# Value products in two halves per tile, and groups of heads that run into each other

## The reference

```
x = x + Attention(layernorm(x));  x = x + FFN(layernorm(x))
Attention: q, k, v from x @ Wqkv + b
  y_softmax = softmax(q k^T / sqrt(16) + causal mask) v        per head, 4096 x 4096
  state_t = retention * state_{t-1} + Gamma * (v_t k_t^T)      a 16 x 16 state per head
  y_stp_t = (W_static + state_t) q_t
  alpha = sigmoid(gelu(x @ gate_w1 + b) @ gate_w2 + b)
  y = alpha * y_softmax + (1 - alpha) * y_stp;  out = y @ out_w + out_b
FFN: fp8-rounded activations and weights, one 256 x 256 product, scale, bias
```

## Time and profile before

| | us |
|---|---|
| median of 3 runs (1871.87 to 1874.48) | 1872.21 |
| profiled execution | 1872.81 |
| its span | 1871.0 |
| TensorE: matmuls in flight | 1672.0 (89%) |
| VectorE busy | 1534.8 (82%) |
| ScalarE busy | 1366.0 (73%) |
| GpSimd busy | 1186.3 (63%) |
| maxima, L1401 | 1215.9 |
| exponentials, L1353 | 1124.3 |
| value products, L1262 | 340.2 + 229.8 |

### The profile page before, as it was taken

One profiled execution on the slowest core, in us unless ns is written; L12 is line 12 of the kernel. 1 busy time (PEld: TensorE's weight loads), 2 busy tenths in 40 slices (PEclk: granted clock), 3 DMA queues, 4 the chain that ended last, 5 costly groups with the idle time before them and its releaser, 6 DMA issues. The chain is left out here.

```text
span 1871.0 us, 37359 instructions
## 1 busy us (share of the span) xinstructions
PE 1672.0 (89%) x13712; PEld 598.9 (32%) x13712; DVE 1534.8 (82%) x1717; ACT 1366.0 (73%) x2835; POOL 1186.3 (63%) x1138
## 2 busy tenths in 40 slices
PE   4997589999999999999999999999999999997745
PEld 2553122232333323223333232233333332322632
DVE  3557888999889899998888999988989999831777
ACT  1552178888888788888877888888878888897333
POOL 2100487777777677777777777777778888770620
PEclk9997589999999999999999999999999999999875
DMA  2774442323123422231224222312341321201702
GB/s 78 234 248 145 111 101 62 82 67 90 57 70 81 102 62 80 66 92 56 69 78 108 62 80 66 92 57 67 81 108 60 94 73 49 74 5 28 256 8 83
DMA packets 115321, 162.75 MB, mean 87 GB/s; under 512 B 30081, under 2 KB 57793, under 8 KB 115137
## 3 DMA queue, kind: packets, MB, share of 16 engines
q1 hardware_dynamic: 112608, 158.74, 29.2%
q10 hardware_dynamic: 2528, 1.64, 0.3%
HBM read 121.87 MB, written 38.01 MB: 85 GB/s over the span
## 5 line engine op out<-in xcount | busy, mean ns | idle before, releaser
L1401 DVE TENSOR_REDUCE pmax<-PS 128x2 f32<-128x1024 f32 (+2 forms) x1120 | 1215.9, 1131 | 131.7 <-PE PS L1205 93.7
L1353 ACT ACTIVATE probs<-PS 128x512 f32<-128x512 f32 (+3 forms) x2304 | 1124.3, 572 | 244.8 <-PE PS L1241 167.4
L1241 PE MATMUL PS<-Q_st,K_st 50*128 50x512 f16 (+3 forms) x1408 | 389.4, 361 | 18.4 <-DVE y_sb L1426 4.8
L1205 PE MATMUL PS<-K_st,Q_st 48*128 48x512 f16 (+3 forms) x1408 | 343.7, 360 | 13.3 <-DVE pmax L1401 11.8
L1262 PE MATMUL PS<-probs,V_g 128*17 128x512 f32 (+3 forms) x2816 | 340.2, 556 | 9.3 <-ACT probs L1353 4.5
L1113 POOL TENSOR_TENSOR v_exp<-v_exp,k_rows 128x512 f32<-128x512 f32 x256 | 320.8, 1280 | 39.1 <-DMA v_exp<-qkv_t 38.5
L1155 POOL TENSOR_TENSOR state<-odd,q_rows 128x514 f32<-128x514 f32 x256 | 281.8, 1133 | 6.1
L1241 PE MATMUL PS<-Q_st,K_first 50*128 50x512 f16 (+3 forms) x896 | 270.6, 378 | 15.7 <-DVE shift L1416 5.2
L1205 PE MATMUL PS<-K_first,Q_st 48*128 48x512 f16 (+1 forms) x832 | 212.4, 399 | 26.0 <-DVE pmax L1401 25.5
L1262 PE MATMUL PS<-probs,V_first 128*17 128x512 f32 (+3 forms) x1792 | 229.8, 585 | 0.0
L1241 PEld LDWEIGHTS PS<-Q_st,K_st 50*128 50x128 f16 x1408 | 105.5, 93 | 369.6 <-ACT probs L1353 306.7
(11 more groups left out here) (170 smaller groups left out, 1460.4 us busy)
## 6 DMA issues: line engine op xcount, KB each, us to landing
v_exp<-qkv_t SPq DMA_DIRECT2D x256, 256.0 KB
qkv_t<-proj SPq DMA_DIRECT2D x24, 512.0 KB, 3.8
qk_parts<-parts SPq DMA_DIRECT2D x16, 512.0 KB, 5.3
Q_st<-qk_parts SPq DMA_DIRECT2D x192, 32.0 KB, 4.0
v_rows<-vaug SPq DMA_DIRECT2D x8, 544.0 KB, 6.1
xin<-x SPq DMA_DIRECT2D x8, 512.0 KB, 6.3
k_rows<-qkv_t SPq DMA_DIRECT2D x16, 256.0 KB, 4.0
q_rows<-qkv_t SPq DMA_DIRECT2D x16, 256.0 KB, 6.0
```

The source lines that it names most:

```text
L1205: mm = pe.matmul(PS[:, bank, 0:width], Q_st[rows, c, pair, j * P:(j + 1) * P], keys[rows, pair, blk * CH:blk * CH + width], start=True, st ...
L1241: mm = pe.matmul(PS[:, bank, 0:CH - r * P], keys[rows, pair, kt * P:(kt + 1) * P], Q_st[rows, c, pair, r * P:CH], start=True, stop=(kt < T ...
L1353: act.activation(probs[:, tile % P_SLOTS, h, 0:CH - r * P], PS[:, step[5], 0:CH - r * P], ACT.Exp, scale=SCORE_SCALE).then_inc(exp_done, 1)
L1401: dve.tensor_reduce(pmax[:, s % 2, pair * TPC + j:GH * TPC:PAIRS * TPC, blk], PS[:, bank:bank + SIDES, 0:width], AX.X, ALU.max).then_inc(m ...
```

## The change

`values` takes a part: 0 is the left 256 columns of the output bank, 1 the right 256, 2 the whole. Plain and scan tiles issue part 0 (`v`) after two scores and two maxima and part 1 (`w`) at the end; burst and lag tiles keep the whole product (`V`). The product is still that of the tile before (`V_LAG` is 1). Only part 0 or the whole waits for the exponentials and for the output bank, and only part 1 or the whole signals; in diagonal tiles a half with no columns issues nothing. The units' steps (U) stand first in a plain tile, no longer behind the first scores. `group_steps` takes what is pending from the group before and hands on its own; only the last group runs dry. SyncE's loop now holds only groups 1 and 2, and turns are counted through the whole program.

```diff
+V_LAG = 1
+WHOLE = 2
-PLAIN_TILE = "SUMMSSMMSV"
+PLAIN_TILE = "USSMMvSSMMw"
 BURST_TILE = "USSMMRMMSSMMV"
-SCAN_TILE = "USSMMRSSV"
+SCAN_TILE = "USSRvSSMMw"
 LAG_TILE = "USSMMVSSMMR"
...
-def group_steps(last):
-    steps, turns, pending = [], [], []
+def group_steps(last, pending, turns, used):
+    steps = []
...
-    def values():
-        s, kt = pending.pop(0)
-        steps.append(("values", 0, s, kt))
+    def values(part):
+        d, s, kt = pending[0]
+        steps.append(("values", d, s, kt, part))
+        if part == 0:
+            return
+        pending.pop(0)
         if kt == KEY_TILES[s] - 1:
-            steps.append(("out_evac", 0, s))
-            turns.append([OUT_LEAD, "out_turn", "out_norm", 0, s])
+            steps.append(("out_evac", d, s))
+            turns.append([OUT_LEAD, "out_turn", "out_norm", d, s])
...
                 elif kind == "V":
-                    if pending:
-                        values()
+                    if len(pending) >= V_LAG:
+                        values(WHOLE)
+                elif kind in "vw":
+                    if len(pending) >= V_LAG:
+                        values("vw".index(kind))
...
-    values()
-    while turns:
-        turns[0][0] = 0
-        turn()
-    return steps
+    if last:
+        while pending:
+            values(WHOLE)
+        while turns:
+            turns[0][0] = 0
+            turn()
+    return steps, ([(d - 1, s, kt) for d, s, kt in pending], [x[:3] + [x[3] - 1, x[4]] for x in turns], used % S_BANKS)
...
-                    def values(g, s, kt):
+                    def values(g, s, kt, part):
...
+                        first, end = max(r * P, PAIR if part == 1 else 0), PAIR if part == 0 else CH
-                        if kt == 0:
+                        if kt == 0 and part != 1:
                             pe.wait_ge(out_evacuated, g * NCH + s + 1)
...
-                        pe.wait_ge(exp_done, g * GH * TILES + GH * (tile + 1) + GH * TILES)
+                        if part != 1:
+                            pe.wait_ge(exp_done, g * GH * TILES + GH * (tile + 1) + GH * TILES)
+                        if first >= end:
+                            return
                         for h in range(GH):
-                            mm = pe.matmul(PS[h * VW:h * VW + VN, O_BANK, r * P:CH], v[:, kt, h * VN:(h + 1) * VN],
-                                           probs[:, tile % P_SLOTS, h, 0:CH - r * P],
-                                           start=(kt == 0), stop=(kt == KEY_TILES[s] - 1))
-                        mm.then_inc(values_done, 1)
+                            mm = pe.matmul(PS[h * VW:h * VW + VN, O_BANK, first:end], v[:, kt, h * VN:(h + 1) * VN],
+                                           probs[:, tile % P_SLOTS, h, first - r * P:end - r * P],
+                                           start=(kt == 0 and part != 1), stop=(kt == KEY_TILES[s] - 1))
+                        if part != 0:
+                            mm.then_inc(values_done, 1)
...
-                    with sp.Fori(0, NG - 1) as group:
-                        walk(group, STEPS, STEP_TURNS, len(FIRST_TURNS), False)
-                    walk(NG - 1, LAST_STEPS, LAST_TURNS, len(FIRST_TURNS), True)
+                    walk(0, STEPS[0], TURNS[0], TURNS_AT[0], False)
+                    with sp.Fori(1, NG - 1) as group:
+                        walk(group, STEPS[1], TURNS[1], (group - 1) * len(TURNS[1]) + TURNS_AT[1], False)
+                    walk(NG - 1, STEPS[NG - 1], TURNS[NG - 1], TURNS_AT[NG - 1], True)
```

More of the change, by code:

```diff
@@ L300, in emptied_before @@
                    if kind != "max"}
-FIRST_STEPS, STEPS, LAST_STEPS = first_steps(), group_steps(False), group_steps(True)
-FIRST_TURNS, STEP_TURNS, LAST_TURNS = turn_numbers(FIRST_STEPS), turn_numbers(STEPS), turn_numbers(LAST_STEPS)
+FIRST_STEPS = first_steps()
+STEPS, left = [], ([], [], 0)
+for group in range(NG):
+    steps, left = group_steps(group == NG - 1, *left)
+    STEPS.append(steps)
+FIRST_TURNS, TURNS = turn_numbers(FIRST_STEPS), [turn_numbers(steps) for steps in STEPS]
+TURNS_AT = [len(FIRST_TURNS) + sum(len(TURNS[n]) for n in range(group)) for group in range(NG)]
+TURN_CREDIT = 2 * NCH
 FIRST_LAGS = 1
 STEP_LAGS = N_SWEEPS
-STEP_TAIL = emptied_before(STEPS, {})[1]
 FIRST_EMPTIED = emptied_before(FIRST_STEPS, {})[0]
-STEP_EMPTIED = emptied_before(STEPS, STEP_TAIL)[0]
-LAST_EMPTIED = emptied_before(LAST_STEPS, STEP_TAIL)[0]
+EMPTIED, tail = [], {}
+for steps in STEPS:
+    found, tail = emptied_before(steps, tail)
+    EMPTIED.append(found)
 def preln_attention_ffn_kernel(nc, x, wqkv, bqkv, out_w, out_b, w_static, lam, gamma, gate_w1,
@@ L1046, in walk @@
                             elif kind == "shift_split":
-                                sp.wait_ge(turn_emptied, group * len(STEP_TURNS) + turns["shift_turn", step[1], s]
-                                           + turns_before + len(STEP_TURNS) + 1)
+                                sp.wait_ge(turn_emptied, turns_before + turns["shift_turn", step[1], s] + TURN_CREDIT + 1)
                                 for side in range(SIDES):
@@ L1056, in walk @@
                             elif kind == "out_norm":
-                                sp.wait_ge(turn_emptied, group * len(STEP_TURNS) + turns["out_turn", step[1], s]
-                                           + turns_before + len(STEP_TURNS) + 1)
+                                sp.wait_ge(turn_emptied, turns_before + turns["out_turn", step[1], s] + TURN_CREDIT + 1)
                                 sp.sem_inc(beats, 1)
@@ L1307, in walk @@
                             elif kind == "values":
-                                values(g, s, step[3])
+                                values(g, s, step[3], step[4])
                             elif kind == "burst":
@@ L1312, in walk @@
                             elif kind == "lag":
-                                if emptied[step[:3]]:
-                                    wait_emptied(group, emptied[step[:3]], turns_before)
+                                wait_emptied(group, emptied[step[:3]], turns_before)
                                 lag(g, s, step[3])
@@ L1383, in _ @@
                     walk(0, FIRST_STEPS)
-                    for group in range(NG - 1):
-                        walk(group, STEPS)
-                    walk(NG - 1, LAST_STEPS)
+                    for group in range(NG):
+                        walk(group, STEPS[group])
                 @block.vector
```

21 lines of the change are left out of this document (11 added, 10 removed).

## The result

The changed kernel takes **1816.62 us** (median of 4 runs, 1814.11 to 1819.28), the kernel before on the same chip 1872.04 (4 runs, 1870.37 to 1874.48): ratio 0.970, interval 0.968 to 0.972, 55 us less. The forecast was 1803, its own range 1785 to 1825. The direction, the place (the middle stage) and the first cause (a ring of latencies that the halves break) came true. What the forecast named as the next limit did not, and its terms were off by more than the 14 us by which the sum was too generous, in both directions.

What follows compares the result with a forecast made beforehand. A ring of latencies through one bank was taken to bound plain tiles. Three groups 45.6, three ends 13.5 and the fourth group 10.6 total 70: 1873 - 70 = 1803 us, own range 1785 to 1825, 8 in 10 1760 to 1858.

Steps and rivals of the forecast that it cites:

- The ring of before: Plain tile: latencies through one score bank, with the long value product among them, set its 2.37 us, not an engine.
- TensorE's price of the halves: Plain tile: two half products and added changes of mode cost TensorE 0.23 us more, 2.18 in all.
- VectorE becomes the bound of a plain tile: Plain tile after the change: VectorE's two maxima, 2.26 us, set it; gain taken as 0.10 a tile, 7.3 a group.
- Bursts, 6.4 a group: Eight burst tiles a group: VectorE's queued work covers the burst, gaining 0.8 us each; 4 in the fourth group.
- Group ends, 4.5 each: Three group ends: running into the next group saves 3.1 us of lost time and 1.4 for the fallen clock.
- Fourth group's end at nothing: End of the fourth group, without maxima: ScalarE is busy for 19.5 of 20 us, so no gain.
- The ring of 2.12: Plain tile, new order: fourth exponential, half, third scores and round again take 2.12 us, under VectorE's 2.26.
- GpSimd does 278 us in a group of 378; it fits in 350: Groups of heads: GpSimd's 278 us of work still fits when a group shortens from 378 to 350 us.
- A: Rival: VectorE is bound everywhere in the groups, 1735 to 1762 us; chance 15%.
- B: Rival: another ring keeps plain tiles at 2.36 us or so, leaving ends and part of bursts, about 1848; chance 15%.
- C: Rival: scalings ahead of the first exponential delay TensorE's queue, slower, 1932 us, or 1877 with half exposed; chance 10%.
- D: Rival: TensorE's time with halves is underrated, plain tiles stay at 2.38 us, 1858 to 1873; chance 5%.

Runs made afterwards that it cites:

- e3: Changed kernel with the value product whole at the end of plain and scan tiles instead of halves: 1952.94 us, 1.043 of the kernel before.
- e6: Changed kernel with the value product whole in mid-tile and taken from two tiles earlier: 1947.19 us, 1.038 of the kernel before.
- e8: Changed kernel with each of VectorE's maxima taken over half the columns only: 1792.91 us, 0.956 of the kernel before.
- e5: Changed kernel, halves kept, with the value product that of two tiles earlier: 1822.01 us, 0.972 of the kernel before.
- e1: Changed kernel with the old tile orders and whole products, only group ends running into the next group: 1864.06 us, 0.996 of the kernel before.
- e2: Changed kernel with halves, but every group run dry at its end as before: 1818.49 us, 0.970 of the kernel before.
- e7: Changed kernel with whole products at the tile's end in the last group once its maxima have run out: 1802.77 us, 0.963 of the kernel before.
- e11: Changed kernel without edits, run once more on another chip: 1812.33 us, 0.967 of the kernel before.
- e4: Changed kernel with the units' steps, scalings included, again behind the first scores of plain tiles: 1823.18 us, 0.972 of the kernel before.

## Why the prediction was right, and where it was wrong

**The ring of before: right.** That the 2.37 us of a plain tile are a ring through one bank with the whole product in it, and that two halves break it, stands by e3 and e6, and by the starts of the scores (0.055 us behind the exponential that frees the bank, in the kernel before as in e3): with whole products the new order gives 2.60, with halves 2.19. VectorE and ScalarE do nearly the same work in all of them (343 and 314 us in a group of e6, 337 and 319 in one after).

**TensorE's price of the halves: right.** 0.23 more a tile, 2.18 in all; the undisturbed tile takes 2.19. Going from scores to maxima costs 0.22, from maxima to a half 0.31 to 0.32. The Trainium skill's rule that a change of tiling mode drains the array ("TensorEngine Tiling (Array Packing)", Key Properties) agrees with the 0.09 in between. It was not a reason against the change: the two added half products with their changes cost 0.23 a tile, and the tile became 0.19 shorter.

**"VectorE becomes the bound of a plain tile": wrong.** The step took 2.26 for VectorE from four maxima in a row, and gave 0.12 at most. The undisturbed tile is at 2.19, below that, and e8, with a third of VectorE's busy time gone, leaves it at 2.19 and the group at 356.1. How VectorE keeps up with 2.19 is argued, not shown: in the row at 673.21 three maxima take 3.49, so two take 2.26 from start to start, while TensorE issues two in 2.19; it would fall behind by part of the banks in reserve, and catch up in longer tiles. The term came out too small: 0.17 a plain tile on the mean instead of 0.10, and over 86 tiles instead of 73. The sign that the prediction had given for being right, plain tiles at 2.26 to 2.30 and VectorE above 94% busy, nearly came (2.29 on the mean, 94.1%), and yet the mechanism was another: a sign that two mechanisms share doesn't tell them apart. Why the mean stays 0.10 above the undisturbed tile is open beyond the scalings: neither e5 nor e8 moved it by more than 0.02.

**Bursts, 6.4 a group: wrong.** The step said that VectorE's queue would be full at the burst. It isn't, since VectorE isn't the bound, and the 3.18 between maxima and the 0.82 idle are unchanged. The burst tile gained nothing, 5.15 before and after. The error hangs on the one before.

**Why the middle groups came out all the same: luck.** Errors cancelled: forecast 7.3 + 6.4 + 1.5 + 4.5 = 19.7. Measured in the second group: 14.8 in the 86 plain tiles, 0 at bursts, 2.7 in the group's last tile, 2.5 in the first three diagonal tiles of the chunks, 1.0 in six tiles with a transposition and 0.3 in lag tiles and at chunk starts; 1.2 lost in last diagonal tiles and 0.1 in scan tiles: 20.0, the group's gain of 19.9 but for rounding. (The 2.7 of the last tile is set against the dry end in the old order; against the dry end with halves the run-over gives 0.8.) A right sum of a group wasn't evidence for its terms.

**Group ends, 4.5 each: wrong by size.** Alone 3.2 (e1), of which the last group gives back 2.6 once; beside the halves 0.8, and about 3.4 in the tiles around the one end where the clock fell (e2). The charge of 1.4 for the fallen clock was for something that need not come. Why the clock falls at a dry end in one case and not in another stays open.

**Fourth group's end at nothing: wrong.** It was costed from ScalarE's 19.5 of 20 us alone. Up to its last maxima the fourth group gained 11.0, near the forecast's 10.6; behind them it lost 9.5, and e7 gives 9.4 back. That is the largest part of the miss. Two steps of the prediction failed here. The ring of 2.12 (fourth exponential, half, third scores) stood in it, and was compared with VectorE's 2.26 only; where there are no maxima it must be compared with ScalarE's 1.91, and is longer. And the wait of a chunk's first half for the evacuated bank was covered by "reserve again"; behind the last maxima there is none, and it cost 3.4 in four tiles, the fallen clock behind it included.

**The list of rings: incomplete.** Only one of the two rings through reused banks was written down. It changed nothing in the forecast (both are 2.16 with halves), but it made e6's expectations wrong.

**First group: 4.7 short.** The step that failed is "GpSimd does 278 us in a group of 378; it fits in 350". As an average it does, at the first group's start it doesn't: GpSimd is busy for 25.59 of 26 us there. The first eight tiles went from 21.9 to 25.3 us where those of the second group went from 20.3 to 19.4; that difference, 4.3, is nearly all of the shortfall. The rest of the first group gained 18.8, the rest of the second 19.1. The wait of 1.86 on GpSimd and the low clock behind it (e11) are read from rows; no experiment took them away by themselves. By e11 one or two of these us change from execution to execution, and what decides that wasn't found.

**The rivals.** A (VectorE bound, to 1762) and B (the tile stays at 2.36) fell. C, slower by exposed scalings, fell: a scaling costs some 0.15 in tiles with one, not the 0.43, and moving it doesn't help (e4); but its mechanism, a scaling ahead of the first exponential that holds up TensorE's queue, did show at the start of the first group. D fell: TensorE's time was rated rightly at 2.18, though it is this time that now sets the undisturbed tile.

## What to carry to other kernels

With n banks in rotation and m products a tile, write down every ring (product k, its reader, product k + n, and the way back), and put the longest instruction into each position in turn: here none of the three positions tried was good, and cutting it was. Then do the same for each stretch in which another engine's work is missing, since a limit that hides beneath it there comes to the surface; and for each stretch in which another engine has more to do than on the average, since a faster start runs into it. An engine that is 94% busy may still not be the bound, and shortening its work is the experiment that tells. Before you compare two executions in a window, align the windows on the same work.

## What wasn't expected of the hardware

The granted clock over the same 26 us at the start of the groups was 0.82 in one execution and 0.87 in another of the same kernel. A drained group end is followed by a clock of 0.75 in the kernel before, but in e2 by 1.00 at two ends, and by 0.77 over 14 us around the third. The value product over 256 columns takes 0.559 us to what follows, over 128 columns 0.346.
